# Cross attention of layer 1: who adds up the exponentials of a head (VectorE's five tiles go to GpSimd and the DMA queue)

## The chip, the cores and the metric

The kernel runs on one core of a Trainium2 chip. The metric is the device time of one execution in microseconds (us), the median of three runs. The engines are named as the profile names them: PE is TensorE's matmul, PEld its weight load, DVE is VectorE, ACT is ScalarE, POOL is GpSimd (its own DMAs are issued from its queue), SP is SyncE (most DMAs are issued from there).

## The reference

A two-layer Perceiver block on 512 tokens of width 512. Each layer has a cross attention over 8192 context rows, a token mixer and a feed-forward part with experts. The change is in the cross attention of layer 1, which has no mask:

```
def _L1_xattn_ref(query, key, value, qpos, kpos, Wq, Wk, Wv, Wo, bo):
    q = (query @ Wq.T).reshape(Bsz, Nq, H, D).transpose(0, 2, 1, 3)
    k = (key @ Wk.T).reshape(Bsz, -1, H, D).transpose(0, 2, 1, 3)
    v = (value @ Wv.T).reshape(Bsz, -1, H, D).transpose(0, 2, 1, 3)
    attn = jnp.einsum('bhqd,bhkd->bhqk', q, k) * SCALE
    attn = jax.nn.softmax(attn, axis=-1)
    x = jnp.einsum('bhqk,bhkd->bhqd', attn, v)
    x = x.transpose(0, 2, 1, 3).reshape(Bsz, Nq, C)
    return x @ Wo.T + bo
```

Here Nq is 512, there are 8192 keys, H is 16 heads of D = 32. The denominator of the softmax is the sum of 8192 exponentials for each query and head; it is this sum whose work is dealt out anew.

## The kernel before, in words

The stages run one behind the other: cross attention of layer 0, a scan, experts, cross attention of layer 1, linear attention, a last feed-forward part. Both cross attentions are one function, `cross_attention`; the one of layer 0 is `masked`, that of layer 1 isn't.

A head is worked off in `PAIRS` = 32 steps. A step makes one **tile of exponentials**: two blocks of 128 keys by 512 queries, so 128 x 1024 numbers. PE writes the scores of a block into one of two PSUM banks (L647), ACT takes the exponential into a buffer (L749), and PE multiplies it with the values in "waves" of three or four blocks (L665). In the same step PE computes the scores of a head that is 36 steps ahead (L622) and DVE takes their row maxima out of PSUM (L803), because the softmax subtracts the maximum. PE's next maxima wait until DVE has freed one of two PSUM pairs (`s_red`). Every engine works off a fixed program, in its order.

The tiles lie in a ring of ten buffers (`n_p` = 10: eight named prob, and two that are halves of xnT). ACT may write a buffer again when the waves have read it and when whoever adds it to the denominator is through (`tile_free`). So whoever adds tile p has to be done before ACT starts tile p + 10.

The denominator of a head is the sum of its 32 tiles, made in four ways, dealt out by `Sums(by_dve, by_pe, by_dma)`; GpSimd gets what is left (`by_pool`):

- DVE adds tiles 0 to 4 into `den_pool` (four instructions, L833 and L836, in its program at steps 3 to 6).
- PE sums six tiles by matmuls with ones (L661).
- GpSimd adds its tiles into the same `den_pool` (L924), and starts only when DVE's are in.
- The others are added by DMA into `den_dma`: GpSimd issues a DMA that copies the first (L910) and DMAs that accumulate the rest (L906). Each waits until the one before it has landed, and GpSimd's queue stands still in that wait.

At the end of a head GpSimd issues one more accumulating DMA, the **merge** (L900), which adds `den_dma` to `den_pool`. It waits for the last add and the last DMA. In the program it stands at step 1 of the next head, and the next head's first DMA waits for its landing. PE then sums `den_pool` over the partitions (`head_out`, L677 to L679) at step 10 of the next head; for the last head it does so behind the output projection's first 24 matmuls (L103).

```
if m == 0:
    e.wait_ge(s_ddve, sums.dve_adds * (h + 1))
else:
    e.wait_ge(s_dpool, sums.pool_done(h, p) - 1)
e.tensor_tensor(den[:], den[:], tile, ALU.add).then_inc(s_dpool, 1)
```

Of the kernel before, what the change touches and what calls it, by code (L numbers as in the profile page):

```python
# [410 lines left out]
PAIRS = KT // 2  # L411
# [92 lines left out]
def cross_attention(k, ctx, q_hi_lo, k_hi_lo, v_heads, wo, w_out, bias, x_rows, comb, scale, masks, attT):  # L504
# [10 lines left out]
    if masked:  # L515
        sums = Sums([0, 1, 2, 3, 4], [], list(range(5, PAIRS - 2, 3)))
    else:
        sums = Sums([0, 1, 2, 3, 4], [12, 15, 18, 21, 24, 27], [7, 10, 13, 16, 19, 22, 25, 29])
    waves = Waves(sums.by_pe)
    q_stack = [k.sbuf(ctx, "q_stack", [QROWS + 2, T], F32R) for _ in range(n_q)]  # L520
    k_ring = k.sbuf(ctx, "k_ring", [QROWS + 2, kring, KC], F32R)
# [419 lines left out]
def l0_cross(k):  # L941
    x_rows = k.i["x"].rearrange("o (i p) d -> p (o i) d", p=P)
    with ExitStack() as outer:
        attT = k.sbuf(outer, "attT", [P, DT, T], F32)
        with ExitStack() as ctx:
            mask_k = k.sbuf(ctx, "mask_k", [P, KT, T], F8)
            comb = k.sbuf(ctx, "comb", [P, DH], F32)
            with ExitStack() as tmp:
# [6 lines left out]
                with k.nc.Block() as block:  # L955
# [14 lines left out]
                    def _(e):  # L970
# [3 lines left out]

            wo = mask_q[:, 0, 0:2 * DT * D].bitcast(F32).rearrange("p (c n) -> p c n", c=DT)
            cross_attention(k, ctx, q.dram, k.k0, k.i["ctx_heads"], wo,
                            k.i["L0_xattn_WoT"].rearrange("(k p) n -> p k n", p=P),
                            k.i["L0_xattn_bo"].rearrange("(o n) -> o n", o=1), x_rows, comb[:], D ** -0.5,
# [3 lines left out]
def l1_cross(k):  # L982
    x_rows = k.dram("x_kept", [P, TT, D])
    with ExitStack() as outer:
        attT = k.sbuf(outer, "attT", [P, DT, T], F32)
        wo = k.sbuf(outer, "w_out", [P, DT, D], F32)
        with ExitStack() as ctx:
            comb = k.sbuf(ctx, "comb", [P, DH], F32)
            with ExitStack() as tmp:
# [7 lines left out]
                with k.nc.Block() as block:  # L997
# [29 lines left out]
                    def _(e):  # L1027
# [3 lines left out]
                        q.pe(e, lambda c: [(wq[:, d, c * P:(c + 1) * P], k.xnT[:, d, :]) for d in range(DT)])  # L1031
                k.block_over()
            cross_attention(k, ctx, q.dram, k.k1, k.v1, wo[:], k.i["L1_xattn_WoT"].rearrange("(k p) n -> p k n", p=P),
                            k.i["L1_xattn_bo"].rearrange("(o n) -> o n", o=1), x_rows, comb[:], DH ** -0.5, None, attT)

# [1860 lines left out]
```

## Time and profile before

| what | value |
|---|---|
| time before, median of 3 runs | 4477.82 us (4474.61 to 4483.54) |
| the profiled execution: its own time | 4484.0 us |
| its span in the trace | 4481.9 us |
| PE busy over the span | 89% |
| DVE / ACT / POOL busy over the span | 67% / 52% / 37% |
| mean granted PE clock | 0.93 |

The shares are means over six stages with different limits. The stage of the change runs from about 2590 to 3656 us of the span, and only its rows say what a change in it is worth. In a row of the timeline the first number is the start in us from the span's start, the second the time until the last of the merged instructions ended, "x2" how many were merged, and the bracket the idle time of the engine ahead of them with what ended it.

### The profile page before, as it was taken

What the parts mean: (1) busy time and instruction counts of PE and PEld (TensorE: products, weight loads), DVE (VectorE), ACT (ScalarE), POOL (GpSimd) and SP (SyncE); (2) the same over time, 40 slices, a digit from 0 to 9 for tenths busy, and PEclk for the clock granted to TensorE, in tenths of its full rate; (3) what the DMA queues carried; (4) which work ended last, traced back from release to release, by engine and by line L of the source; (5) the groups of instructions that cost most, each with busy time, mean ns of one, the idle gap of its engine ahead of it and who ended that gap; (6) DMA issues with size and microseconds to landing.
All of it is one profiled execution on the core that took longest, in us unless ns stands there. A gap on an engine that the chain in (4) does not pass through costs nothing. (4 is left out here: it accounts for less than half of the span.)

```text
span 4481.9 us, 50984 instructions
## 1 busy us (share of the span) xinstructions
PE 3975.0 (89%) x17680; PEld 2213.4 (49%) x17680; DVE 2993.9 (67%) x3608; ACT 2351.9 (52%) x3611; POOL 1667.8 (37%) x984
## 2 busy tenths in 40 slices
PE   7995899999999686678999779999999988769997
PEld 6883344444443341147777434444444335447775
DVE  4333878777785359936777567777778644467776
ACT  2221577777777333313676426666666631337674
POOL 0001487778878425400000036666566630000000
PEclk9997899999999779889999869999999988789998
DMA  8998566666666200022888546666666540318886
GB/s 310 328 336 273 150 153 152 155 154 148 156 149 144 80 14 0 0 85 113 302 301 302 203 132 154 152 154 152 140 151 144 120 99 26 79 59 305 304 300 227
DMA packets 301550, 751.69 MB, mean 168 GB/s; under 512 B 55793, under 2 KB 89329, under 8 KB 268016
## 3 DMA queue, kind: packets, MB, share of 16 engines
q1 hardware_dynamic: 245136, 560.20, 37.1%
q0 software_dynamic: 47456, 171.46, 19.0%
q10 hardware_dynamic: 8704, 16.78, 1.1%
q8 instruction: 142, 2.33, 0.2%
q14 instruction: 112, 0.92, 0.1%
HBM read 484.23 MB, written 98.37 MB: 130 GB/s over the span
## 5 line engine op out<-in xcount | busy, mean ns | idle before, releaser
L749 ACT ACTIVATE prob<-psum 128x512 f32<-128x512 f32 x1552 | 891.7, 595 | 430.7 <-PE psum L647 393.7
L647 PE MATMUL psum<-q_stack,k_ring 98*128 98x512 f32 x2048 | 1006.1, 510 | 19.8 <-ACT prob L749 14.4
L924 POOL TENSOR_TENSOR den_pool<-den_pool,prob 128x1024 f32<-128x1024 f32 x372 | 937.2, 2519 | 220.2 <-DVE den_pool L836 184.7
L622 PE MATMUL psum<-k_ring,q_stack 96*128 96x512 f32 x2048 | 691.7, 422 | 106.3 <-DVE row_max L807 36.1
L803 DVE TENSOR_REDUCE row_max<-psum 128x1 f32<-128x1024 f32 x512 | 615.3, 1220 | 238.0 <-PE psum L622 235.0
L807 DVE CUSTOM_DVE_ANT_0 psum<-psum,mask_q 128x1024 f32<-128x1024 f32 x512 | 627.3, 1233 | 206.5 <-PE psum L622 191.2
L647 PEld LDWEIGHTS psum<-q_stack,k_ring 98*128 98x128 f32 x2048 | 395.2, 194 | 620.7 <-ACT prob L749 274.7
L1891 DVE TENSOR_TENSOR weight_lo<-weight_raw,weight_hi 128x2048 fp32r<-128x2048 f32 x240 | 546.9, 2289 | 163.2 <-ACT weight_hi L1834 162.9
L665 PE MATMUL psum<-prob,x 128*32 128x512 f32 x3104 | 515.7, 610 | 0.9 <-ACT prob L749 0.9
L622 PEld LDWEIGHTS psum<-k_ring,q_stack 96*128 96x128 f32 x2048 | 394.1, 200 | 213.7 <-issue 84.2
L1834 ACT ACTIVATE weight_hi<-weight_raw 128x2048 fp32r<-128x2048 f32 x240 | 454.4, 1916 | 43.2 <-DMA weight_raw<-in_L_ffn_w 25.3
L749 ACT ACTIVATE xnT<-psum 128x512 f32<-128x512 f32 x496 | 288.6, 594 | 129.3 <-PE psum L647 120.3
L1747 POOL DMA_DIRECT2D y_slots<-xnT x30 | 16.4, 547 | 878.8 <-ACT xnT L1856 878.8
L924 POOL TENSOR_TENSOR den_pool<-den_pool,xnT 128x1024 f32<-128x1024 f32 x124 | 311.8, 2514 | 53.6 <-DVE den_pool L836 43.4
L646 PE MATMUL psum<-mask_k,ident_big 128*128 128x512 fp8e4 x768 | 300.6, 391 | 12.8 <-ACT prob L749 8.8
L1333 PE MATMUL psum<-dB_u,ident 128*128 128x512 f32 x256 | 156.1, 709 | 100.0 <-DVE dB_u L1308 99.8
L906 POOL DMA_DIRECT2D den_dma<-prob x180 | 155.9, 866 | 171.2 <-ACT prob L749 93.8
L1294 POOL TENSOR_TENSOR dB_u<-delta_u,B_all 128x2048 f32<-128x2048 f32 x32 | 144.2, 4512 | 200.9 <-POOLq L1176 113.6
L103 PE MATMUL psum<-weight_hi,hidden_T_hi 128*128 128x512 f32 x480 | 199.8, 416 | 3.8 <-DVE weight_lo L1891 3.8
L665 PE MATMUL psum<-xnT,x 128*32 128x512 f32 x992 | 202.2, 611 | 0.7 <-ACT prob L749 0.7
L103 PE MATMUL psum<-weight_hi,slot_x_hi 128*128 128x512 f32 x480 | 201.4, 420 | 0.0
L103 PE MATMUL psum<-weight_hi,hidden_T_lo 128*128 128x512 f32 x480 | 188.7, 393 | 0.0
(422 smaller groups left out, 6385.6 us busy)
## 6 DMA issues: line engine op xcount, KB each, us to landing
weight_raw<-in_L_ffn_w SPq DMA_DIRECT2D x120, 1024.0 KB, 6.7
den_dma<-prob POOLq DMA_DIRECT2D x204, 512.0 KB, 4.9
k_ring<-k_hi SPq DMA_DIRECT2D x1024, 64.0 KB, 2.2
weight_raw<-in_L_ffn_Wu SPq DMA_DIRECT2D x60, 1024.0 KB, 7.2
weight_raw<-in_L_ffn_Wd SPq DMA_DIRECT2D x60, 1024.0 KB, 4.9
den_dma<-xnT POOLq DMA_DIRECT2D x68, 512.0 KB, 4.9
k_ring<-k_lo SPq DMA_DIRECT2D x512, 64.0 KB, 2.4
ctxT<-in_ctxT SPq DMA_DIRECT2D x16, 1024.0 KB, 9.5
```

The source lines that it names most:

```text
L103: ins = e.matmul(out, lhsT, rhs, start=start and n == 0, stop=stop and n == len(terms) - 1)
L622: ins = e.matmul(max_banks(q)[:, a * KC:(a + 1) * KC], q_stack[h % n_q][0:QROWS, i * P:(i + 1) * P], k_ring[0:QROWS, (n + a) % kring, :], ...
L646: e.matmul(k.bank(b % 2), k.ident_big[:], masks[1][:, t, :], start=True, stop=False)
L647: e.matmul(k.bank(b % 2), k_ring[:, n % kring, kt * P:(kt + 1) * P], q_stack[h % n_q][:], start=not masked, stop=True, skip_group_check=ma ...
L665: ins = e.matmul(vbank[n * DH:(n + 1) * DH, :], v_buf[t // 16][:, t % 16 * DH:(t % 16 + 1) * DH], prob[(PAIRS * h + t // 2) % n_p][:, t % ...
L749: e.activation(prob[b // 2 % n_p][:, b % 2, :], k.bank(b % 2), ACT.Exp, scale=scale).then_inc(s_exp, 1)
L803: e.reduce_max(out, max_banks(q), AXIS_X).then_inc(s_red, 1)
L807: e.tensor_tensor_reduce(out=max_banks(q), in0=max_banks(q), in1=masks[0][:, i, 2 * c2 * KC:2 * (c2 + 1) * KC], scale=1.0, scalar=-3.0e38, ...
L924: e.tensor_tensor(den[:], den[:], tile, ALU.add).then_inc(s_dpool, 1)
L1333: e.matmul(y(m), k.ident[:], db_of(n), start=st == 0, stop=st == NST - 1).then_inc(s_sum, 1)
L1834: e.activation(hi[q % RING][:], raw[q % RAW][:], ACT.Copy).then_inc(s_whi, 1)
L1891: e.tensor_tensor(lo[q % RING][:], raw[q % RAW][:], hi[q % RING][:].bitcast(F32), ALU.subtract).then_inc(s_wlo, 1)
```

## The change

The denominator's tiles of a head in layer 1 are dealt out anew. The layer 0 line is as it was.

```diff
@@ -515,7 +515,7 @@
     if masked:
         sums = Sums([0, 1, 2, 3, 4], [], list(range(5, PAIRS - 2, 3)))
     else:
-        sums = Sums([0, 1, 2, 3, 4], [12, 15, 18, 21, 24, 27], [7, 10, 13, 16, 19, 22, 25, 29])
+        sums = Sums([], [12, 15, 18, 21, 24, 27], list(range(5, PAIRS - 2, 3)))
```

By tile this is:

| who | before | now |
|---|---|---|
| DVE | 0 1 2 3 4 | none |
| PE | 12 15 18 21 24 27 | the same |
| DMA | 7 10 13 16 19 22 25 29 | 5 8 11 14 17 20 23 26 29 |
| GpSimd | 5 6 8 9 11 14 17 20 23 26 28 30 31 (13 adds) | 0 1 2 3 4 6 7 9 10 13 16 19 22 25 28 30 31 (16 adds) |

With no tile left to DVE, GpSimd's first add takes tiles 0 and 1 together (L917), so 17 tiles are 16 adds.

GpSimd's queue at the beginning of the second head of layer 1, from the merge of the first head on. Before:

```order
L900 DMA den_pool<-den_dma 128x1024
L924 TENSOR_TENSOR den_pool<-den_pool,prob 128x1024
L924 TENSOR_TENSOR den_pool<-den_pool,xnT 128x1024
L910 DMA den_dma<-xnT 128x1024
L924 TENSOR_TENSOR den_pool<-den_pool,prob 128x1024 x2
L906 DMA den_dma<-prob 128x1024
L924 TENSOR_TENSOR den_pool<-den_pool,prob 128x1024
L906 DMA den_dma<-prob 128x1024
```

And now:

```order
L900 DMA den_pool<-den_dma 128x1024
L917 TENSOR_TENSOR den_pool<-prob 128x1024
L924 TENSOR_TENSOR den_pool<-den_pool,prob 128x1024 x3
L910 DMA den_dma<-prob 128x1024
L924 TENSOR_TENSOR den_pool<-den_pool,xnT 128x1024 x2
L906 DMA den_dma<-prob 128x1024
L924 TENSOR_TENSOR den_pool<-den_pool,prob 128x1024 x2
L906 DMA den_dma<-prob 128x1024
L924 TENSOR_TENSOR den_pool<-den_pool,prob 128x1024
L906 DMA den_dma<-prob 128x1024
```

Four adds instead of two now stand between the merge and the first DMA, and two adds stand behind each of the first two DMAs; from there on one add and one DMA alternate up to the last DMA of the head, in both kernels.

DVE's queue in the same head, as the difference of the two:

```order
-L803 TENSOR_REDUCE row_max<-psum 128x1 x5
-L833 TENSOR_TENSOR den_pool<-prob 128x1024
-L803 TENSOR_REDUCE row_max<-psum 128x1
-L836 TENSOR_TENSOR den_pool<-den_pool,prob 128x1024
-L803 TENSOR_REDUCE row_max<-psum 128x1
-L836 TENSOR_TENSOR den_pool<-den_pool,prob 128x1024
-L803 TENSOR_REDUCE row_max<-psum 128x1
-L836 TENSOR_TENSOR den_pool<-den_pool,xnT 128x1024
-L803 TENSOR_REDUCE row_max<-psum 128x1 x5
+L803 TENSOR_REDUCE row_max<-psum 128x1 x13
```

The four adds that stood between maxima are gone, and nothing takes their place. The queues of PE and ACT are the same row for row.

## Rows read from the trace of the kernel before

**Rows 1.** The page: busy time by engine.
```profile
PE 3975.0 (89%) x17680; PEld 2213.4 (49%) x17680; DVE 2993.9 (67%) x3608; ACT 2351.9 (52%) x3611; POOL 1667.8 (37%) x984
```

**Rows 2.** Waits, 2700 to 3400 us: who for whom, us, times, longest.
```profile
ACT prob L749 <- PE psum L647: 164.7, 196, 2.8
...
POOL den_pool L924 <- DVE den_pool L836: 99.0, 12, 11.0
...
PE psum L622 <- DVE row_max L803: 15.5, 16, 1.9
...
ACT prob L749 <- POOL den_pool L924: 1.7, 2, 0.8
```

**Rows 3.** Timeline of DVE and PE near 2966 us: the wait for DVE.
```profile
2966.65 4.61 DVE L803 TENSOR_REDUCE row_max<-psum 128x1 f32<-128x1024 f32 x4
...
2965.74 0.70 PE L622 MATMUL psum<-k_ring,q_stack 96*128 96x512 f32 x2 [0.95 <-DVE row_max L803]
```

**Rows 4.** Timeline of ACT, one head and the turn to the next.
```profile
2966.71 0.60 ACT L749 ACTIVATE xnT<-psum 128x512 f32<-128x512 f32 x1 [1.24 <-PE psum L647]
...
2981.97 2.49 ACT L749 ACTIVATE prob<-psum 128x512 f32<-128x512 f32 x4 [0.83 <-PE psum L647]
...
2998.34 2.49 ACT L749 ACTIVATE prob<-psum 128x512 f32<-128x512 f32 x4 [0.83 <-PE psum L647]
...
3010.14 2.56 ACT L749 ACTIVATE prob<-psum 128x512 f32<-128x512 f32 x4 [0.31 <-PE psum L647]
```

**Rows 5.** Timeline of POOL, the same head, from its first add on.
```profile
2966.89 4.89 POOL L924 TENSOR_TENSOR den_pool<-den_pool,prob 128x1024 f32<-128x1024 f32 x2 [8.92 <-DVE den_pool L836]
2971.72 0.58 POOL L910 DMA_DIRECT2D den_dma<-prob  x1
...
2977.16 0.86 POOL L906 DMA_DIRECT2D den_dma<-prob  x1
2977.78 2.66 POOL L924 TENSOR_TENSOR den_pool<-den_pool,prob 128x1024 f32<-128x1024 f32 x1
...
2989.97 0.87 POOL L906 DMA_DIRECT2D den_dma<-prob  x1 [3.71 <-ACT prob L749]
...
2996.09 0.87 POOL L906 DMA_DIRECT2D den_dma<-xnT  x1 [2.84 <-DMA den_dma<-prob]
...
3006.58 0.87 POOL L906 DMA_DIRECT2D den_dma<-prob  x1 [2.14 <-ACT xnT L749]
...
3013.00 0.87 POOL L906 DMA_DIRECT2D den_dma<-xnT  x1 [0.60 <-ACT prob L749]
3013.59 5.22 POOL L924 TENSOR_TENSOR den_pool<-den_pool,prob 128x1024 f32<-128x1024 f32 x2
3019.11 0.88 POOL L900 DMA_DIRECT2D den_pool<-den_dma  x1 [0.30 <-POOL den_pool L924]
```

**Rows 6.** Timeline of POOL: another head's DMAs, and the first and the fifteenth merge.
```profile
2717.20 0.88 POOL L900 DMA_DIRECT2D den_pool<-den_dma  x1 [0.30 <-POOL den_pool L924]
...
2735.24 0.85 POOL L906 DMA_DIRECT2D den_dma<-prob  x1
...
2763.47 0.87 POOL L906 DMA_DIRECT2D den_dma<-prob  x1 [2.04 <-ACT prob L749]
...
3570.86 0.88 POOL L900 DMA_DIRECT2D den_pool<-den_dma  x1 [0.30 <-POOL den_pool L924]
```

**Rows 7.** Time to landing of the denominator's DMAs, layer 1 (2646 to 3656 us).
```profile
DMA to landing us min/median/max: 2.9/5.0/7.2
```

**Rows 8.** Timeline of all engines at the stage's end.
```profile
3619.02 1.09 ACT L749 ACTIVATE prob<-psum 128x512 f32<-128x512 f32 x2 [0.58 <-PE psum L647]
...
3623.79 0.88 POOL L900 DMA_DIRECT2D den_pool<-den_dma  x1 [0.30 <-POOL den_pool L924]
...
3631.65 0.62 PE L677 MATMUL psum<-o_sb,comb 128*32 128x512 f32 x1
```

## The prediction

> **What bounds the kernel now.** I read the page first, then the waits of the stage, then the timelines of one head engine by engine. On the page PE is busy 89% of the span and GpSimd 37% [rows 1], which says little here: GpSimd works only in the cross attentions. The waits over 700 us of the stage show ACT waiting for PE's scores, 196 times, 164.7 us in all, while ACT waited for GpSimd only twice, 1.7 us [rows 2]. So the pace of a head is that of the loop between PE and ACT, and the adds were in time. A head takes 61.0 us on average: fourteen heads lie between the first and the fifteenth merge, (3570.86 - 2717.20) / 14 [rows 6].
>
> Two things touch that loop. One is DVE. Its four adds stand between maxima, so it falls behind at the start of a head: at 2966.65 us it works off four maxima without a break, and PE waited 0.95 us for it just before [rows 3]. ACT, fed by PE, then stood idle 1.24 us [rows 4]. Over the 700 us PE waited 15.5 us in 16 waits for these maxima [rows 2].
>
> The other is GpSimd's queue, which is close behind. It waits for DVE at the start of each head (8.92 us in this one [rows 5], 99.0 us in twelve [rows 2]) and then works without being ahead again. In the middle of a head it waits for DMAs, not for work. From the DMA at 2977.16 to that at 3006.58 there are five intervals of three tiles each, 29.42 us or 5.9 us apiece [rows 5]; an earlier head has 28.23 us for the same five (2735.24 to 2763.47), 5.6 us apiece [rows 6]. One add of 2.7 us, 0.6 us behind the DMA [rows 5], fills only 3.3 us of that. The rest is the wait for the DMA before to land, of which the median is 5.0 us [rows 7]. How near that is to stopping ACT: tile 16 of this head was ready at about 2983.3 (the first half of four exponentials from 2981.97), its DMA was issued at 2989.97, the next one at 2996.09, and ACT starts tile 26 in its buffer at about 2999.5, in the four exponentials from 2998.34 [rows 4, 5]. So there are about 4 us of room at this tile. At the end of the head GpSimd's last add is over at 3018.8 while tile 31 was ready at about 3011.4 (half of the four from 3010.14): it is 7.4 us late [rows 4, 5].
>
> **What the change does, part by part.**
>
> *DVE's adds go.* Four instructions a head leave DVE, and with them the wait at the head's start. I value it by ACT's idle time there, 1.2 us [rows 4], in the 15 heads beside which maxima are still computed (the last has none left): 18 us off. From below this is 0 (the wait moves to another partner of the loop); from above, 15.5 us and more in 700 us are 1.4 us a head, some 21 us [rows 2]. I take 18, the row of ACT, since ACT sets the steps.
>
> *GpSimd's head gets longer.* I add up its queue from merge to merge, on the assumption that it is late all the time and waits only for its own adds and DMAs. The four adds from the merge to the first DMA: 0.6 us behind the merge as behind any DMA, two adds 5.2 us (13.59 to 18.81), two more 4.9 us, a gap of 0.1: 10.8 us [rows 5]. The merge's own landing fits under them, as a DMA lands in 5.0 us [rows 7]. The first DMA is a copy; to the second, with two adds between, 5.4 us (2971.72 to 2977.16). From the second to the third, two adds behind 0.6 us: 5.8 us. Then six intervals with one add each, from tile 11 to 29, at the pace of landings: between 5.6 and 5.9 us, I take 5.75, together 34.5 us [rows 5, 6]. From the last DMA to the merge, with two adds: 6.1 us (3013.00 to 3019.11) [rows 5]. The sum is 62.6 us.
>
> Without GpSimd the head would take 61.0 - 1.2 = 59.8 us. So GpSimd loses 2.8 us in every head, 42 us in 15. Before, its queue was set back each head by the wait for DVE and yet ended level, since that wait holds work that DVE did for it. Now nothing takes it back: lateness adds up until the ring of ten is full. Some 6 us of it are free (4 us of room at tile 16 [rows 4, 5], a little more at others). From about the third head ACT then waits for `tile_free`, and PE with it. That is 42 - 6 = 36 us.
>
> *The tail.* The merge of the last head stands at 3623.79, 3.7 us behind the last exponential (3619.02 + 1.09); PE is busy with the output projection until it needs it at 3631.65 [rows 8]. If GpSimd is as late as the ring lets it, 7.4 + 6 = 13.4 us, the merge is issued at about 3620.1 + 13.7 = 3633.8 and lands 5 us later, at about 3639; PE waits some 7 us. Then follow the reciprocal and the rest of the projection as now. I take 8 with the start of `head_out`.
>
> *The DMAs.* One more of 512 KB a head; all of the DMAs of the denominator run one at a time, so they don't collide with each other. Their landing times vary beside the loads of keys and values (2.9 to 7.2 us [rows 7]), and one more in ten doesn't change that much; I price it at nothing and keep it in the range.
>
> The sum against the profiled execution's own time: 4484 - 18 + 36 + 8 = 4510 us. The median of the runs stands 6 us below that execution, so 4504 us.
>
> A rule is to be weighed here. The rows show an accumulating DMA of 512 KB landing after 5.0 us in the median, and the shortest at 2.9 us [rows 7]. The Trainium skill (DMA: Bandwidth & Descriptors, section on the anatomy of one DMA) fits a DMA issued by GpSimd as 2.0 us plus its bytes over 436 KB a us, which gives an estimate of 3.2 us; the shortest here is near it, the median isn't. By that rule the six intervals would be short, no chain would bind, and the time would be that of the first rival below.
>
> **The rivals.**
>
> *GpSimd keeps up: faster.* If the interval between DMAs comes to 5.3 us or less, the cycle is at most 62.6 - 6 x 0.45 = 59.9 us, no longer than the head, and what is left is DVE's 18 us, less a few us in the tail: 4484 - 18 + 3 - 6 = 4463 us. For it speaks that the median landing of 5.0 us with the 0.5 us until the next issue would be 5.5, below the means of the heads; against it that both heads shown have 5.6 and more, and that the average counts in a chain, not the median. It decides at about 5.5 us: then 60.9 or 61.1 us a cycle cost about what DVE gives back. Chance 0.12.
>
> *They cancel.* With intervals of 5.5 us the cycle is 61.1 us, 1.3 over the head, 20 us in 15 heads, less 6 of room, plus some 5 in the tail, less 18: 4484 + 1 - 6 = 4479 us. Chance 0.15.
>
> *It gets worse than my sum.* DVE's wait moves elsewhere and gives nothing, or the intervals come to 6.0 us, as single ones here do (2989.97 to 2996.09 is 6.1 [rows 5]): 1.5 us more a head, 22 us more, 4526 us; both together 4544. Chance 0.2.
>
> That the change doesn't do what it says is out: the queues above show it.
>
> **How the numbers follow.** My own case has a chance of 0.53 and gives 4504 us, by itself from 4488 to 4518. A measurement of this kernel can tell some 0.2%, 9 us, from no change. Each 0.1 us in the DMA's interval is worth 0.6 to 0.7 us a head, 10 us in all; from 5.5 to 6.0 us this is 4479 to 4530. The range of 8 in 10 runs from 4476 to 4532 us. Faster by over 0.2% is the first rival, 0.12; within 0.2% the second, 0.15; slower the rest, 0.73.
>
> **What would show it.** In the profile after: DVE's adds in layer 1 gone, and PE's waits for row_max L803 with them, or else the 18 us are wrong. ACT waits for den_dma's landings and for den_pool on GpSimd, not at all in the first heads and 2 to 4 us a head from the third or fourth on, and merges 62 to 63 us apart. GpSimd 13 us late at the heads' ends instead of 7. PE idle before L677 of the last head for some 8 us. Layer 0 unchanged. The prediction is wrong if DMA to DMA takes under 5.5 us when GpSimd is late, if the four adds at the head's start are much quicker than 2.5 us each beside a DVE that no longer adds, or if PE's granted clock, which no row here ties to such short pauses, falls in them so far that PE becomes the bound again.

## The result, and the profile after

| | median of 5 | lowest to highest |
|---|---|---|
| before | 4478.0 us | 4474.61 to 4483.54 |
| after | 4500.93 us | 4497.96 to 4509.97 |

The ratio is 1.0052 with a 95% interval of 1.0038 to 1.0067: slower by 23 us, where 4504 us was forecast. The span of the profiled execution is 4496.2 us, 14.3 us above that of before. The two traces part already ahead of the stage (layer 1's first head turn stands at 2645.74 us before and at 2640.27 us after); from that turn to the last head's L677 the stage takes 985.9 us before and 1005.7 us after, 19.8 us more.

The page of the kernel after, busy time by engine:

```profile
PE 3975.5 (88%) x17680; PEld 2216.0 (49%) x17680; DVE 2941.8 (65%) x3544; ACT 2344.9 (52%) x3611; POOL 1797.6 (40%) x1048
```

Beside [rows 1], DVE has 64 instructions and 52 us less, GpSimd 64 instructions and 130 us more: its 16 x 3 more adds and 16 more DMAs. PE has the same work, is busy for the same time to 0.5 us (3975.0 and 3975.5 us), and so has a smaller share: what the change costs is idle time of PE and not slower matmuls, and PE's clock, 0.928 on the mean against 0.930, isn't the cause. By the shares alone nothing is near its limit but PE.

The waits after, 2700 to 3400 us, which answer to [rows 2]:

```profile
ACT prob L749 <- PE psum L647: 115.5, 134, 3.4
POOL den_dma L906 <- DMA den_dma<-prob: 86.4, 37, 3.0
ACT prob L749 <- DMA den_dma<-prob: 51.4, 30, 3.1
...
POOL den_dma L906 <- DMA den_dma<-xnT: 23.1, 10, 3.0
...
ACT xnT L749 <- DMA den_dma<-xnT: 7.8, 5, 2.4
PE psum L622 <- DVE row_max L803: 7.3, 7, 2.3
```

Two things carry the finding. One is new: ACT waits 35 times, 59.2 us, for the landing of a DMA that adds a tile, because the tile's buffer is the next that it writes. The other has grown: GpSimd's waits for the DMA before (both rows together 109.5 us in 47 times) were 45.8 us in 17 before:

```profile
POOL den_dma L906 <- DMA den_dma<-prob: 41.5, 15, 3.8
...
POOL den_dma L906 <- DMA den_dma<-xnT: 4.3, 2, 2.3
```

GpSimd's wait for DVE (99.0 us) is gone, PE's for the maxima is halved. The 59.2 us are not the loss: in the same 700 us ACT waits 57.6 us less for PE's scores (L749, both rows), as a wait for a buffer takes the place of a wait for scores. The loss is read from the distance of the heads.

The timeline of POOL after, one head from merge to merge:

```profile
3081.06 0.88 POOL L900 DMA_DIRECT2D den_pool<-den_dma  x1 [0.33 <-POOL den_pool L924]
3081.65 2.71 POOL L917 TENSOR_TENSOR den_pool<-prob 128x1024 f32<-128x1024 f32 x1
3084.50 4.89 POOL L924 TENSOR_TENSOR den_pool<-den_pool,prob 128x1024 f32<-128x1024 f32 x2
3089.54 2.37 POOL L924 TENSOR_TENSOR den_pool<-den_pool,xnT 128x1024 f32<-128x1024 f32 x1
3091.86 0.58 POOL L910 DMA_DIRECT2D den_dma<-xnT  x1
...
3097.31 0.86 POOL L906 DMA_DIRECT2D den_dma<-prob  x1
...
3103.05 0.86 POOL L906 DMA_DIRECT2D den_dma<-prob  x1
...
3131.15 0.87 POOL L906 DMA_DIRECT2D den_dma<-prob  x1 [1.88 <-DMA den_dma<-prob]
3131.74 2.67 POOL L924 TENSOR_TENSOR den_pool<-den_pool,prob 128x1024 f32<-128x1024 f32 x1
3136.74 0.88 POOL L906 DMA_DIRECT2D den_dma<-prob  x1 [2.32 <-DMA den_dma<-prob]
3137.32 5.21 POOL L924 TENSOR_TENSOR den_pool<-den_pool,prob 128x1024 f32<-128x1024 f32 x2
3142.99 0.88 POOL L900 DMA_DIRECT2D den_pool<-den_dma  x1 [0.46 <-POOL den_pool L924]
```

Read against the sum of the prediction: merge to first DMA 10.80 us (forecast 10.8), to the second 5.45 (5.4), to the third 5.74 (5.8), six intervals 33.69 or 5.6 each (34.5, 5.75 each), last DMA to merge 6.25 (6.1). Together 61.93 us, where 62.6 was forecast. In this head the queue doesn't wait for ACT once: it is late all the time.

How late can be read in every head from the timelines of ACT and POOL, as the time from the end of a head's last exponential (tile 31) to the issue of its merge. In heads 1 to 16 it is 7.1, 11.1, 13.6, 14.3, 7.5, 11.6, 14.3, 14.4, 5.1, 10.3, 12.6, 14.2, 14.4, 14.1, 18.3 and 15.2 us; before, it lay between 3.7 and 7.9. It grows by 2 to 4 us a head until it stands at about 14, where the ring is full: in heads 3, 4, 7, 8 and from 12 on ACT starts most of a DMA's buffers 0.1 us behind its landing. Twice it falls back. In heads 5 and 9, and in 13 too (every fourth head, in all runs), DVE also divides the outputs of four heads (eight instructions more) and holds up PE's maxima; such a head took 67.2 and 69.8 us after, part of it at a lower granted clock (0.95 and 0.93 on the mean of the head), and even with two accumulators 61.0 us instead of 58.9.

The first and the fifteenth merge after, in the timeline of POOL:

```profile
2709.79 0.88 POOL L900 DMA_DIRECT2D den_pool<-den_dma  x1 [0.30 <-POOL den_pool L924]
...
3582.43 0.88 POOL L900 DMA_DIRECT2D den_pool<-den_dma  x1 [0.30 <-POOL den_pool L924]
```

That is 62.33 us a head against 60.98 in [rows 6].

And the end of the stage after, all engines:

```profile
3625.02 1.09 ACT L749 ACTIVATE prob<-psum 128x512 f32<-128x512 f32 x2
...
3641.32 0.88 POOL L900 DMA_DIRECT2D den_pool<-den_dma  x1 [0.30 <-POOL den_pool L924]
3646.01 1.03 PE L677 MATMUL psum<-o_sb,comb 128*32 128x512 f32 x1 [8.29 <-DMA den_pool<-den_dma]
```

The last merge now stands 15.2 us behind the last exponential instead of 3.7 [rows 8], and PE, done with its projection, waits 8.29 us for it.

### The profile page after: what moved, and what is told of

Same layout as the page of the kernel before. It is cut to its first block and busy times, and to the rows that moved or that the text cites. A ratio compares the mean times of both kernels' runs of the same rounds, so it can differ in the third digit from the quotient of the medians.

```text
span 4496.2 us, 50985 instructions
## 1 busy us (share of the span) xinstructions
PE 3975.5 (88%) x17680; PEld 2216.0 (49%) x17680; DVE 2941.8 (65%) x3544; ACT 2344.9 (52%) x3611; POOL 1797.6 (40%) x1048
## 5 line engine op out<-in xcount | busy, mean ns | idle before, releaser
L749 ACT ACTIVATE prob<-psum 128x512 f32<-128x512 f32 x1552 | 887.4, 594 | 445.3 <-PE psum L647 316.5
L924 POOL TENSOR_TENSOR den_pool<-den_pool,prob 128x1024 f32<-128x1024 f32 x398 | 1004.2, 2523 | 60.7 <-DVE den_pool L836 32.1
L749 ACT ACTIVATE xnT<-psum 128x512 f32<-128x512 f32 x496 | 287.4, 594 | 127.5 <-PE psum L647 104.7
L924 POOL TENSOR_TENSOR den_pool<-den_pool,xnT 128x1024 f32<-128x1024 f32 x130 | 328.6, 2527 | 25.8 <-DVE den_pool L836 16.8
L906 POOL DMA_DIRECT2D den_dma<-prob x193 | 167.3, 867 | 193.9 <-DMA den_dma<-prob 114.3
L103 PE MATMUL psum<-weight_hi,slot_x_lo 128*128 128x512 f32 x480 | 188.5, 393 | 0.0
```

The source lines that it names most:

```text
L103: ins = e.matmul(out, lhsT, rhs, start=start and n == 0, stop=stop and n == len(terms) - 1)
L749: e.activation(prob[b // 2 % n_p][:, b % 2, :], k.bank(b % 2), ACT.Exp, scale=scale).then_inc(s_exp, 1)
L906: e.dma_start(den_dma[:], tile, accum_op=ALU.add).then_inc(s_ddma, 16)
```

## The experiments

All were run in two sets; each ratio is to the kernel before on the same chip in the same set (median 4475.39 us in the first set, 4477.17 in the second), so ratios are compared, not medians of different sets.

| run | median us | ratio to before, 95% interval |
|---|---|---|
| DVE's tiles left out | 4458.33 | 0.9956 (0.9942 to 0.997) |
| only the DMA's list changed | 4479.73 | 1.0007 (0.9994 to 1.002) |
| two accumulators for the DMAs | 4454.3 | 0.995 (0.9931 to 0.9968) |
| ring of twelve | 4503.94 | 1.0066 (1.0044 to 1.0088) |
| DVE adds three tiles | 4465.4 | 0.9974 (0.9963 to 0.9986) |
| after, tile 4 left out | 4466.63 | 0.998 (0.9966 to 0.9994) |
| two accumulators, PE sums four | 4442.05 | 0.9922 (0.9903 to 0.9941) |
| two accumulators, PE sums two | 4514.16 | 1.0088 (1.0068 to 1.0108) |

**What DVE's adds cost by themselves.** From the kernel before:

```diff
-        sums = Sums([0, 1, 2, 3, 4], [12, 15, 18, 21, 24, 27], [7, 10, 13, 16, 19, 22, 25, 29])
+        sums = Sums([], [12, 15, 18, 21, 24, 27], [7, 10, 13, 16, 19, 22, 25, 29])
+        sums.by_pool = [p for p in sums.by_pool if p > 4]
+        sums.pool_adds = len(sums.by_pool) - 1
```

> Before, but nobody adds tiles 0 to 4 of a head in layer 1 (they are missing from the denominators); PE, DMA and GpSimd keep their other tiles. This is the change's saving on DVE alone. My theory (DVE's four adds hold up PE's maxima by 1.2 us a head in 15 heads, and GpSimd's longer queue costs the rest): 4478 - 18 = 4460 us, head after head 58.9 instead of 60.1 us apart, no wait of ACT for GpSimd or a DMA. Rival A (DVE's adds lie beside other work and cost nothing): 4478 us.

The ratio 0.9956 is 20 us (13 to 26). The turn of two heads in the timeline of ACT (its instruction that writes the row maxima into `q_stack`, once a head):

```profile
2947.40 0.59 ACT L730 ACTIVATE q_stack<-psum 2x512 fp32r<-2x512 f32 x1
...
3006.27 0.59 ACT L730 ACTIVATE q_stack<-psum 2x512 fp32r<-2x512 f32 x1
```

58.87 us in this head, as expected, where an ordinary head before took 60.1 us. It isn't the mean: three of the fifteen, those with DVE's division, took 62.3 to 64.5 us, and the mean from the first turn (2649.91) to the last (3546.63) is 59.8 us, against 61.1 before. Rival A falls: DVE's burst was on the path, and ACT's idle time of 1.2 us was the right measure of it. This run also takes one add from GpSimd, so it bounds DVE's saving from above; GpSimd's lateness held up nobody before but for 1.7 us in 700 [rows 2], so that add is nearly free.

**The DMA's list by itself.** From the kernel before:

```diff
-        sums = Sums([0, 1, 2, 3, 4], [12, 15, 18, 21, 24, 27], [7, 10, 13, 16, 19, 22, 25, 29])
+        sums = Sums([0, 1, 2, 3, 4], [12, 15, 18, 21, 24, 27], list(range(5, PAIRS - 2, 3)))
```

> Before with DVE's five tiles kept and only the DMA's list changed to that of the change (nine DMAs at tiles 5, 8, ... 29; GpSimd has 12 adds). My theory (a chain of GpSimd's work longer than a head): DVE's adds do GpSimd's first four in parallel, so from DVE's last add to the merge GpSimd needs 4.9 + 5.8 + 6 x 5.75 + 6.1 = 51.3 us and comes out level: 4478 us, within 5. Rival B (the ninth DMA and its traffic are what costs): most of the loss appears, 4495 us or more, and ACT waits for den_dma.

No change, to within the interval's 9 us. The ninth DMA, which also takes one add from GpSimd, its traffic and its place are free as long as DVE does the first five tiles: DVE's adds run beside GpSimd's work at the end of the head before and its wait for the merge. Rival B falls.

**Two accumulators.** After, in layer 1 with two `den_dma` taken in turn, each with its own semaphore (the core of the edit; the first DMA of each still copies, and `tile_free` and `head_out` wait for the counts that belong to it):

```diff
-                if m > 0:
-                    e.wait_ge(s_ddma, 16 * (sums.dma_done(h, p) - 1))
-                    e.dma_start(den_dma[:], tile, accum_op=ALU.add).then_inc(s_ddma, 16)
+                a, done = sums.dma_done(h, p, n_acc)
+                if m >= n_acc:
+                    e.wait_ge(s_ddma[a], 16 * (done - 1))
+                    e.dma_start(den_dma[a][:], tile, accum_op=ALU.add).then_inc(s_ddma[a], 16)
...
-                    if p == 1 and h > 0:
-                        merge(h - 1)
+                    if p in (1, 3)[:n_acc] and h > 0:
+                        merge(h - 1, p // 2)
```

> After with two den_dma accumulators in layer 1 that the DMAs take in turn, so that a DMA waits for the one before the last, and with a second merge at step 3. GpSimd's adds are those of after. My theory (GpSimd stands still for the landing of each DMA, 5.1 us): with two under way the six intervals come down to about 3.4 us, GpSimd's head to some 50 us, it is never late, DVE's saving is left: 4460 us, and about 3 more for the second merge at the very end, 4463 us. Rival C (the DMAs are bound by what the 16 engines and SBUF can move, so two at once take twice as long each): intervals stay at 5.7 us, 4500 us. Rival D (GpSimd's adds themselves are too many): 4495 to 4500 us with ACT waiting for den_pool on GpSimd.

0.995: against after this is 46 us, with the same adds, the same tiles moved by DMA and one merge more. The median is 9 us below the 4463 us expected; the interval reaches that of the run with DVE's tiles left out, and the two aren't told apart. The timeline of POOL, two DMAs near the start of a head with the add between them, and a later add:

```profile
2971.76 0.89 POOL L912 DMA_DIRECT2D den_dma<-prob  x1
2972.37 2.69 POOL L930 TENSOR_TENSOR den_pool<-den_pool,prob 128x1024 f32<-128x1024 f32 x1
2974.69 1.21 POOL L912 DMA_DIRECT2D den_dma<-prob  x1
...
2987.36 2.37 POOL L930 TENSOR_TENSOR den_pool<-den_pool,prob 128x1024 f32<-128x1024 f32 x1 [2.27 <-ACT prob L752]
```

While it is late (10 us of adds at the head's start) GpSimd issues its next DMA 2.93 us behind the one before, where after took 5.6. So it catches up within the head, and from then on it waits for ACT's tiles, as a queue with room does. Rivals C and D fall: neither the bytes nor the adds by themselves were the limit, but the adds together with the landing of one DMA at a time.

**A longer ring.** After, with twelve tile buffers:

```diff
-    n_q, n_p = 3, 7 if masked else 10
-    kring = 22 if masked else 36
+    n_q, n_p = 3, 7 if masked else 12
+    kring = 22 if masked else 32
```

> After with twelve tile buffers instead of ten (and 32 key buffers instead of 36, to make room). My theory (GpSimd's head is longer than the others' head, so it is late by more and more, whatever the ring holds): the ring fills one or two heads later and PE's head_out, which waits for the merge, takes the ring's place; 4498 us, within 6 of after. Rival E (GpSimd could keep up on average, and ten buffers are only too few for landings that scatter from 4 to 7 us): the two buffers take the waits away, 4465 to 4480 us.

It gained nothing (1.0066 against after's 1.0052, the intervals overlap). The ring of keys had to be made shorter for it, so a gain of a few us that this took back isn't excluded. Its waits, same 700 us:

```profile
ACT attT L765 <- PE psum L679: 34.7, 12, 4.6
...
ACT prob L749 <- DMA den_dma<-prob: 16.2, 9, 3.7
...
PE psum L677 <- DMA den_pool<-den_dma: 14.6, 8, 2.5
```

ACT's wait for the DMAs fell from 51.4 to 16.2 us, and PE's wait for the merge in `head_out`, 14.6 us in 8 times, took its place, with ACT behind it. The merges stand 62.8 us apart on the mean of fifteen distances, against 62.1 after. A queue that is too slow on average isn't helped by a buffer. Rival E falls.

**Three tiles for DVE.** From the kernel before:

```diff
-        sums = Sums([0, 1, 2, 3, 4], [12, 15, 18, 21, 24, 27], [7, 10, 13, 16, 19, 22, 25, 29])
+        sums = Sums([0, 1, 2], [12, 15, 18, 21, 24, 27], [7, 10, 13, 16, 19, 22, 25, 29])
```

> Before with DVE adding only tiles 0 to 2 of a head in layer 1 (two adds instead of four); GpSimd takes 3 and 4 (15 adds), PE and DMA keep theirs. My theory (GpSimd's queue costs only once its own head exceeds the 58.9 us that the others need): its head is 0.6 + four adds 10.2, then 5.4, then 5 x 5.7, 6.1 and 6.1, together some 57 us, so it costs nothing, and half of DVE's burst is gone, which takes away between half and all of the 1.2 us a head: 4458 to 4468 us. Rival (any tile moved from DVE to GpSimd costs, since GpSimd's add takes twice DVE's): 4485 us or more.

0.9974, 12 us faster than before (6 to 17). Two of the tiles cost GpSimd little and free DVE. The timeline of ACT has its heads at this pace:

```profile
2939.59 0.59 ACT L728 ACTIVATE q_stack<-psum 2x512 fp32r<-2x512 f32 x1
...
2998.52 0.59 ACT L728 ACTIVATE q_stack<-psum 2x512 fp32r<-2x512 f32 x1
```

58.93 us, the whole saving in this head. The median shows 8 us less of a saving than that of the run with the tiles left out, which is at the edge of the intervals. In the traces the stage, from the first turn to the last head's L677, is 6.7 us longer here: 2.4 of them are PE's wait for the last merge, and what takes the rest, in the heads, isn't settled.

**One add less.** After, with tile 4 left out:

```diff
         sums = Sums([], [12, 15, 18, 21, 24, 27], list(range(5, PAIRS - 2, 3)))
+        sums.by_pool = [p for p in sums.by_pool if p != 4]
+        sums.pool_adds = len(sums.by_pool) - 1
```

> After with tile 4 of a head added by nobody in layer 1 (it is missing from the denominators): one GpSimd add of 2.5 us less between the merge and the first DMA, nothing else. My theory (GpSimd's head of 62 us against 58.9): it comes down to 59.5 us, about level with the others, so nearly all of the loss over DVE's saving goes at once, for one add in sixteen: 4466 us (4460 to 4472). Rival F (each GpSimd add costs its share, beside or ahead of the others): a sixteenth of the loss, 4497 to 4500 us.

4466.63 us, as expected. One add in sixteen takes away 0.998 against 1.0052, 32 us of the 43 that GpSimd's queue had cost. Over 15 heads that is 2.1 us for an add of 2.5: nearly one to one, which is what the longest queue looks like. Some 6 us of the 32 lie in the tail, where PE waits 2.45 us for the last merge instead of 8.29. Rival F falls. GpSimd's cycle is 59.6 us here (fifteen merges' distances), a little over an ordinary head of 58.9 but under the mean of 59.8, so its lateness still grows within four heads and is taken back in the fourth: it is the mean head, the long ones included, that GpSimd's cycle has to be compared with.

**With room, more tiles for the DMAs.** Two accumulators, PE with four tiles, then with two:

```diff
-        sums = Sums([], [12, 15, 18, 21, 24, 27], list(range(5, PAIRS - 2, 3)))
+        sums = Sums([], [12, 18, 21, 27], [5, 8, 11, 14, 15, 17, 20, 23, 24, 26, 29])
```

> The kernel with two accumulators, with two of PE's six tiles given to DMA (eleven DMAs and two merges a head; GpSimd's adds unchanged; PE has 18 waves a head instead of 19). If the queue of GpSimd has the room that my theory gives it (some 50 of 58.9 us) and PE is the bound again: one wave less, 1 us a head, 4455 - 16 = 4439 us. Rival (the DMA engines, busy 0.65 of the time before, now stretch every landing): 4455 us or more, with landings above 6 us and ACT waiting for them.

4442.05 us: a wave of PE less a head is worth its 1 us, as PE is the bound again (an ordinary head takes 57.9 us in the trace instead of 58.9). This version beats both kernels, by 0.8% and 1.3%.

```diff
-        sums = Sums([], [12, 15, 18, 21, 24, 27], list(range(5, PAIRS - 2, 3)))
+        sums = Sums([], [15, 24], [5, 8, 11, 12, 14, 17, 18, 20, 21, 23, 26, 27, 29])
```

> As the one before with four of PE's six tiles given to DMA (thirteen DMAs and two merges a head, 17 waves). If PE is the bound: 4455 - 32 = 4423 us. If the DMA engines are, which fifteen transfers of 512 KB a head beside the loads (about 0.9 of the engines' time by the share that nine have) make likelier than in the run before: landings of 7 us and more, ACT waiting for them, 4450 us or more. I expect something between, 4435 us.

4514.16 us: a clear miss. I had expected a value between the two cases. The landings aren't at 7 us either: the accumulating DMAs have a median of 6.2. Its waits, 2700 to 3400 us:

```profile
ACT attT L768 <- PE psum L681: 60.4, 11, 8.0
PEld psum L679 <- issue: 47.4, 11, 6.5
...
PE psum L679 <- DMA den_pool<-den_dma: 37.8, 11, 5.7
```

In every one of eleven heads PE waits in `head_out` for a merge, and ACT behind it, 5.5 us each time, where ACT waited 1.5 us a time there after (17.9 us in 12). It isn't `tile_free` that ACT waits for, as the rival had it. The timeline of POOL at the head's end shows why:

```profile
3013.76 0.88 POOL L912 DMA_DIRECT2D den_dma<-prob  x1
3017.55 0.86 POOL L912 DMA_DIRECT2D den_dma<-prob  x1 [2.92 <-DMA den_dma<-prob]
...
3026.89 0.88 POOL L905 DMA_DIRECT2D den_pool<-den_dma  x1 [0.30 <-POOL den_pool L930]
...
3033.58 0.88 POOL L905 DMA_DIRECT2D den_pool<-den_dma  x1 [0.86 <-POOL den_pool L930]
```

Two merges follow each other 6.7 us apart, one behind the landing of the other, at the end of a queue with thirteen DMAs. The second lands too late for step 10.

PE's granted clock falls with these waits. The same 700 us with eleven DMAs and with thirteen:

```profile
2700.00:3400.00 700.00, 686.10 (x3431) 304.88 (x3432) 503.29 (x456) 467.12 (x816) 583.26 (x349) 1.00 0.83 193
2700.00:3400.00 700.00, 658.93 (x3098) 291.82 (x3090) 474.42 (x418) 434.62 (x759) 559.49 (x345) 0.94 0.85 195
```

The number behind GpSimd's busy time is the granted clock, 1.00 and 0.94. Behind the wait of 4.61 us that ends at 3038.29 it stands at 0.50, the lower level (1.2 GHz), until 3044. The two heads that keep 1.00 take 57.6 and 57.0 us, and the mean is 62.6. Of the 5 us between them PE's waits for the merge are 3.4 (37.8 us in 11), and the rest goes with the clock, as far as these rows tell: PE is busy for 60.5 us in a head at 0.92 where it is for 56.3 at 1.00. Whether this head could be had with the merges in another place wasn't tried.

## Why the prediction was right, point by point

*DVE's burst, 18 us off.* Right. 20 us by the run that leaves the tiles out, and its mean head is 59.8 us, as the sum had it. PE's waits for the maxima at the heads' starts, 0.97 us in each of the twelve heads of the 700 us, are gone, as they had to be. The seven that are left after (7.3 us) all stand in the two heads in which DVE divides.

*GpSimd's head of 62.6 us.* Right: 61.9 in the head shown, 62.3 on the mean. The reading under it holds too: the bracket of the DMA at 2989.97 names ACT [rows 5], but its tile had been ready for 6.7 us, so what it waited for was the DMA before. Its largest term, the six intervals at 5.75 us, was a little high: 5.6 in the head shown, and 34.05 us or 5.68 apiece on the mean of the fourteen heads from the first merge to the fifteenth (the other terms 10.8, 5.5, 5.9 and 6.1 us). The mean of intervals that were themselves waits for landings was the right number to take; 5.5, from the median landing, would have given no change. The rule of 2.0 us plus bytes (an estimate of 3.2 us), which the prediction had weighed from the Trainium skill (DMA: Bandwidth & Descriptors, the section on the anatomy of one DMA), would have given a gain. The trace doesn't agree with it for an accumulating DMA. The landings of the accumulating DMAs after, for layer 1:

```profile
DMA to landing us min/median/max: 4.4/4.9/9.5
```

None lands in under 4.4 us, and before none did either. The prediction read the shortest, 2.9 us [rows 7], as an accumulating one's, and it is a copy's: that row mixes both kinds. No term of the sum hangs on it. Only the first DMA of a head, which copies, comes near to the rule:

```profile
DMA to landing us min/median/max: 2.9/3.6/5.2
```

*Lateness that adds up, 36 us in the heads.* Right in kind and size. GpSimd's loss altogether is 23 + 20 = 43 us, 8 of them in the tail, so 35 in the heads. The traces say the same: from the first turn to the last head's L677 the stage takes 1005.7 us after and 963.1 without DVE's tiles, 42.7 us less. The ring was full from the third head on and GpSimd some 14 us late there, as forecast. What the prediction didn't have is that the heads aren't alike: it spread the loss evenly, at 2 to 4 us a head, while ACT waits up to 14 us in a head with a full ring and hardly at all behind heads 5 and 9. The sum comes out all the same, because GpSimd was late in every head and its cycle set the mean. ACT's waits for `den_pool` on GpSimd, which were forecast beside those for the landings, don't appear in the 700 us. The two runs that attack the chain (two accumulators, one add less) each take away most of it. The ninth DMA alone costs nothing, and the longer ring gives nothing back.

*The tail, 8 us.* Right: 8.29 us of wait before L677. I hadn't reckoned with the matmuls behind it, which take 1.03 us instead of 0.62 [rows 8].

*The DMAs' traffic at nothing.* Right, to within 9 us: 1.0007 with the ninth DMA alone.

*The sum.* Forecast -18 + 36 + 8 = +26, measured +23. No term of it was off by more than some 2 us, so no two large errors made up for each other. But the interval was known no better than 5.6 to 5.9 us, and each 0.1 us of it was worth 10 us in the sum; that it was hit to 0.07 us is in part luck.

## What to carry to other kernels

Before work is moved to an engine that looks idle by its share (37% here), add up that engine's queue over one period of the loop, waits for its own DMAs included, and compare it with the period. Compare it with the mean period, long rounds included. Here a chain of 5 us landings filled the queue, and 62.3 against 59.8 us a head decided all. Where such a chain binds, two of its links under way at once can help: a second accumulator was worth 46 us here, while a longer ring only moved the wait. Near the crossing a single instruction of 2.5 us was worth nearly itself, and below it two adds more cost little (8 us in the medians), so such a change is worth a try one tile at a time.

## What the runs showed of the hardware

Two accumulating DMAs under way at once cost each other little with nine tiles a head: the landings went from 4.9 us in the median to 5.1 in the run with two accumulators (row below). With eleven tiles they were at 5.8 and with thirteen at 6.2, while the mean share of the DMA engines over 700 us went from 0.74 to 0.83 and 0.85.

```profile
DMA to landing us min/median/max: 4.4/5.1/7.2
```

PE's granted clock can fall behind a short wait. Before, PE was busy until a wait for DVE of 0.98 us in one head; then, from 3273.4 to 3275.4 us, the granted clock was 0.50, the lower of its two levels (1.2 GHz), and a wave of eight matmuls took 1.94 us:

```profile
3272.49 0.70 PE L622 MATMUL psum<-k_ring,q_stack 96*128 96x512 f32 x2 [0.98 <-DVE row_max L803]
3273.03 0.51 PE L647 MATMUL psum<-q_stack,k_ring 98*128 98x512 f32 x1
3273.47 1.94 PE L665 MATMUL psum<-prob,x 128*32 128x512 f32 x8
```

In another head, behind a wait of 0.95 us, the granted clock stayed at 1.00 and the same wave took 1.07 us:

```profile
2966.60 1.07 PE L665 MATMUL psum<-prob,x 128*32 128x512 f32 x8
```

So it isn't each such wait that does this, and what decides it no run here tells. The head with the lower clock took 61.6 us instead of 60.1. The prediction, which tied no such pause to the clock, had this row in the trace of before; over the whole change it cost nothing, as PE's busy time shows. In the run with two accumulators, where the waits at the heads' starts are gone, the granted clock was 1.00 in every head from the second to the fifteenth.
